# Attention stage: who copies the value product out of PSUM, VectorE or ScalarE

## The chip, the cores and the metric

The kernel runs on one core of a Trainium2 chip. The metric is the device time of one execution in microseconds (us). Engine names: TensorE (PE; its weight loads are a row of their own, PEld), VectorE (DVE), ScalarE (ACT), GpSimd (POOL) and SyncE (SP). A difference is told from none here from 0.2% on.

## The reference

Four graph layers run one after the other on x, of shape 128 batches x 128 nodes x 128 channels, each as `x = x + layer(relu(layernorm(x)))`. The second is the attention layer, the one that the change touches:

```python
qkv = x @ Wqkv
q, k, v = jnp.split(qkv, 3, axis=-1)
scores = jnp.einsum('btd,bsd->bts', q, k) * scale + adj_mask
scores = jnp.where(causal, scores, NEG)
attn = jax.nn.softmax(scores, axis=-1)
y = jnp.einsum('bts,bsd->btd', attn, v)
return y @ Wo
```

The first layer is a graph convolution with four small LSTMs, the third mixes three weight matrices by parts of the adjacency, the fourth is an edge attention.

## The kernel before, in words

The whole of x stays in SBUF. The attention stage works on 128 batches in 8 turns of 16 (`TURNS`, `NB`), each turn in 4 groups of 4 batches (`W1`, `QB`), so there are 32 groups. Query and key weights are multiplied ahead of time into one matrix `m_qk`, value and output weights into `w_vo`. All data of this stage are fp32. A group goes through these steps:

- `HT`: TensorE transposes the four normalised tiles (L820) into PSUM; ScalarE copies them with a relu to `hT1`.
- `QK`: the query product with `m_qk` (L826, one matmul of 512 columns); ScalarE copies it to `hmT`.
- `VAL`: the value product, `hT1` with `w_vo`, four matmuls (L831) into PSUM bank 2; it is copied to `val`. This copy is the subject.
- `SCORE`: four score matmuls (L837); VectorE adds the masked adjacency (L751) and takes the negated row maximum (L755).
- `EXP`: ScalarE takes four exponentials with row sums (L798).
- `PT`: TensorE transposes the exponentials (L843); ScalarE copies them to `probT`.
- `OUT1`: four matmuls of `probT` with `val` (L850); VectorE divides by the row sums and adds to x (L769, L775).
- `STATS` and `APPLY`: VectorE takes statistics of the turn after (L762, L107), GpSimd makes scale and shift and the normalised tiles (L727 to L740).

The three plain copies on ScalarE share one line, L786. The trace counts a matmul of fp32 data twice where it isn't a transpose, so four value matmuls are 8 in it.

Each engine runs the rounds in an order written out by hand. `IN_ROUND` is the order of TensorE, ScalarE and GpSimd, `ON_VECTOR` that of VectorE. An entry (step, d) means that in round r the step is done for group r - d. So in one round TensorE does HT of group r, PT of r-3, QK, VAL and SCORE of r-1 and OUT1 of r-3, and the EXP of a round is for group r-2. Engines are in step by semaphores only: `b_vp` says that the value product is there, `b_v` that it has been copied (the value product of the next round waits for it, since there is one bank, and so does OUT1 two rounds later), `b_e` that the exponentials are there (PT of the next round waits for it).

Of the kernel before, what the change touches and what calls it, by code (L numbers as in the profile page):

```python
# [21 lines left out]
def sync_names(nc, ctx, names):  # L22
    return {n: ctx.enter_context(nc.semaphore(n)) for n in names.split()}


def four_layers(nc, x_in, adj, adjT, Wg0, bg0, Wg1, bg1, WihT, WhhT, bihT, bhhT, WqkvT, Wo, W2, bias2,
# [11 lines left out]
    with ExitStack() as ctx:  # L38
# [65 lines left out]
        def norm_aggr(k, n, done):  # L104

            for j in range(k, k + n):
                nc.vector.bn_aggr(mv[:, j], stats[:, j]).then_inc(done, 1)  # L107
# [10 lines left out]
        def turn_start(i):  # L118

            return 0 if isinstance(i, int) and i == TURNS else i * NB  # L120
# [15 lines left out]
        def relu_norm(act, i, g, k, n):  # L136
# [3 lines left out]
            for j in range(g * GB + k, g * GB + k + n):  # L140
# [36 lines left out]
        S = sync_names(nc, ctx, "ld_e ld_x0 ld_lstm ld_w ld_x1 ld_x pool_made dve_made w_high w_low pool_link dve_link "  # L177
                                "act_link pe_srt pe_w pe_b0 pe_adj")
        with nc.Block() as block:

            @block.sync
            def _(sp):
                ends = ((ends_row[:, 0], src_row.to_broadcast([P, E])), (ends_row[:, 1], dst_row.to_broadcast([P, E])),
                        (ends_col[:, 0], src_col), (ends_col[:, 1], dst_col))
                for dst, s in ends:
                    sp.dma_start(dst, s).then_inc(S["ld_e"], 16)
                sp.dma_start(x[:, 0:NB, :], x_in[0:NB].rearrange("b t c -> t b c")).then_inc(S["ld_x0"], 16)
                for dst, s in ((w_raw[:, 0], WihT), (w_raw[:, 1], WhhT), (b_ih[:], bihT), (b_hh[:], bhhT)):
                    sp.dma_start(dst, s).then_inc(S["ld_lstm"], 16)
                for dst, s in ((adj_sb[:], adj), (adjT_sb[:], adjT), (w_g[:, 0], Wg0), (w_g[:, 1], Wg1),  # L190
                               (b0_col[:], bg0), (b1_bc[:], bg1.to_broadcast([P, P])), (a_sb[:], a_col),
                               (wqkvT[:], WqkvT.rearrange("(k d) c -> d k c", d=P)), (wo_sb[:], Wo),
                               (w2_sb[:], W2.rearrange("k f o -> f k o")),
                               (w_lv[:], WlvT), (w_out[:], WoutT),
                               (bias2_bc[:], bias2.to_broadcast([P, P]))):
                    sp.dma_start(dst, s).then_inc(S["ld_w"], 16)
                for i in range(1, TURNS):
                    sp.dma_start(x[:, i * NB:(i + 1) * NB, :],
                                 x_in[i * NB:(i + 1) * NB].rearrange("b t c -> t b c")).then_inc(
                                     S["ld_x1" if i == 1 else "ld_x"], 16)  # L200
# [253 lines left out]
        with nc.Block() as block:  # L454
# [121 lines left out]
            def _(pe):  # L576
# [48 lines left out]
                def item(i, g, n, more, before):  # L625
# [39 lines left out]
                    else:  # L665
# [13 lines left out]
        val = tmp("val", [P, W1, QB, C])  # L679
# [5 lines left out]
        S = sync_names(nc, ctx, "b_stats b_aggr b_var b_nmean b_rstd b_shift b_hn b_hTp b_hT b_qp b_q b_vp b_v b_sp b_s b_max b_e b_pTp "  # L685
                                "b_pT b_op b_inv b_o")
        HT, PT, QK, VAL, SCORE, OUT1, EXP, STATS, APPLY = range(9)


        IN_ROUND = [(HT, 0), (PT, 3), (QK, 1), (VAL, 1), (EXP, 2), (SCORE, 1), (STATS, 0), (OUT1, 3), (APPLY, 1)]  # L690
        ON_VECTOR = [(OUT1, 4), (STATS, 0), (VAL, 1), (SCORE, 1)]

        def pipeline(stage, beside):

# [18 lines left out]
        def bank(what, g):  # L713
            return ps[:, BANK[what][g % 2]]

        def by4(ap, n=QB):
            return ap.rearrange("p (b t) -> p b t", b=n)

        with nc.Block() as block:
# [25 lines left out]
            @block.vector  # L745
            def _(dve):
                def stage(i, what, g, more, before):
                    count = i * W1 + g + 1
                    if what == SCORE:
                        dve.wait_ge(S["b_sp"], count)  # L750
                        nc.vector.tensor_tensor(prob[:, g], by4(bank(SCORE, g)),  # L751
                                                adj_causal[:].unsqueeze(1).to_broadcast([P, QB, T]),
                                                ALU.add).then_inc(S["b_s"], 1)
                        dve.wait_ge(S["b_s"], count)
                        nc.vector.tensor_reduce(nmax[:, g * QB:(g + 1) * QB], prob[:, g], AXX, ALU.max,  # L755
                                                negate=True).then_inc(S["b_max"], 1)
                    elif what == VAL:
                        dve.wait_ge(S["b_vp"], count)
                        nc.vector.tensor_copy(val[:, g], by4(bank(VAL, g))).then_inc(S["b_v"], 1)
                    elif what == STATS:  # L760
                        for j in range(g * QB, (g + 1) * QB):
                            nc.vector.bn_stats(stats[:, j], x[:, turn_start(i + 1) + j]).then_inc(S["b_stats"], 1)  # L762
                        dve.wait_ge(S["b_stats"], count * QB)
                        if i > 0:
                            dve.wait_ge(S["b_shift"], count - W1)
                        norm_aggr(g * QB, QB, S["b_aggr"])
                    elif what == OUT1:
                        dve.wait_ge(S["b_e"], count)
                        nc.vector.reciprocal(rinv[:, g * QB:(g + 1) * QB], rsum[:, g * QB:(g + 1) * QB]).then_inc(  # L769
                            S["b_inv"], 1)  # L770
                        dve.wait_ge(S["b_op"], count)
                        dve.wait_ge(S["b_inv"], count)
                        for b in range(QB):
                            xs = x[:, i * NB + g * QB + b]
                            ins = nc.vector.scalar_tensor_tensor(xs, bank(OUT1, g)[:, b * C:(b + 1) * C],  # L775
                                                                 rinv[:, g * QB + b:g * QB + b + 1], xs,
                                                                 ALU.mult, ALU.add)
                        ins.then_inc(S["b_o"], 1)

                pipeline(stage, ON_VECTOR)  # L780

            @block.scalar
            def _(act):
                def copy(sem, count, dst, src, done, func=ACT.Copy):
                    act.wait_ge(sem, count)
                    nc.scalar.activation(dst, by4(src), func).then_inc(done, 1)  # L786

                def stage(i, what, g, more, before):
                    count = i * W1 + g + 1
                    if what == HT:  # L790
                        copy(S["b_hTp"], count, hT1[:, g], bank(HT, g), S["b_hT"], ACT.Relu)
                    elif what == QK:
                        copy(S["b_qp"], count, hmT[:, g], bank(QK, g), S["b_q"])
                    elif what == EXP:
                        act.wait_ge(S["b_max"], count)
                        for b in range(QB):
                            n = g * QB + b
                            ins = nc.scalar.activation(prob[:, g, b], prob[:, g, b], ACT.Exp, bias=nmax[:, n:n + 1],  # L798
                                                       accum_out=rsum[:, n:n + 1])
                        ins.then_inc(S["b_e"], 1)  # L800
                    elif what == PT:
                        copy(S["b_pTp"], count, probT[:, g], bank(PT, g), S["b_pT"])

                pipeline(stage, IN_ROUND)

            @block.tensor
            def _(pe):
# [5 lines left out]
                def stage(i, what, g, more, before):  # L813
# [31 lines left out]
                    elif what == OUT1:  # L845
                        pe.wait_ge(S["b_pT"], count)
                        pe.wait_ge(S["b_v"], count)
                        if count > 2:
# [14 lines left out]
        S = sync_names(nc, ctx, "c_stats c_aggr c_var c_rstd c_nmean c_shift c_hn c_hTp c_hTh c_hTl c_wp c_hw c_xb "  # L863
                                "c_own c_op c_o")
# [8 lines left out]
        with nc.Block() as block:  # L873
# [87 lines left out]
            def _(pe):  # L961
                def stage(i, what, g, more, before):
# [20 lines left out]
                    elif what == OUT2:  # L983
# [3 lines left out]
                        for k in range(2):  # L987
# [27 lines left out]
        S = sync_names(nc, ctx, "d_stats d_aggr d_var d_rstd d_nmean d_shift d_hn d_hTp d_hT d_xqp d_xvp d_xqh d_xql "  # L1015
                                "d_xv d_zp d_rl d_lr d_lgp d_logd d_logp d_log")
# [7 lines left out]
        with nc.Block() as block:  # L1024
# [78 lines left out]
            def _(pe):  # L1103
# [21 lines left out]
                for n in range(NG):  # L1125
# [23 lines left out]
                    if n == 0:  # L1149
# [15 lines left out]
        S = sync_names(nc, ctx, "e_lg e_fb e_m e_sub e_exp e_exTp e_ex e_denp e_inv e_att e_xvh e_xvl e_vp e_va "  # L1165
                                "e_yp e_y e_op e_o e_st")
# [187 lines left out]
```

## Time and profile before

| | |
|---|---|
| median of 3 runs | 1310.18 us (1309.94 to 1312.72) |
| the profiled execution | 1309.45 us |
| span of its trace, first to last instruction | 1307.6 us |
| busy over the span: TensorE, VectorE, ScalarE, GpSimd | 91%, 77%, 62%, 32% |
| attention stage, hT transposes of group 0 to the next stage's first | 737.3 to 889.8 us |

The profile is of one execution. Times in its rows are in us from the span's start unless they are called ns. The idle time in brackets is that of the engine ahead of the instruction, with an arrow to what ended it. The share of busy time over the whole span is a mean over four stages with different limits, so the attention stage has to be read by itself.

### The profile page before, as it was taken

The page shows a single profiled execution, that of the slowest core. Times are in us where ns is not written, and L with a number is a line of the kernel's source. Part 1 is how long each engine was busy: PE and PEld are TensorE (multiplying, and loading weights), DVE is VectorE, ACT ScalarE, POOL GpSimd, SP SyncE. Part 2 cuts the span into 40 slices and gives each one's busy share as a digit, 9 for nine tenths or more (in the row PEclk, how much of TensorE's full clock was granted, in tenths as well). Part 3 has the DMA queues.
Part 4 walks back from the last instruction along what each step waited for, and adds up shares of the span by engine and source line. Part 5 has one row for each costly group of instructions (what it writes and reads, how often), then busy time and mean ns, then how long its engine had stood idle before and what let it go on. Part 6 is the DMA issues. An engine that isn't in the chain of part 4 may idle for free. (4 is left out here: it accounts for less than half of the span.)

```text
span 1307.6 us, 24530 instructions
## 1 busy us (share of the span) xinstructions
PE 1192.5 (91%) x7808; PEld 1024.9 (78%) x7808; DVE 1010.0 (77%) x2796; ACT 812.9 (62%) x1804; POOL 412.6 (32%) x779
## 2 busy tenths in 40 slices
PE   2889999899899998998999799998999899968998
PEld 1678788787787886877878688886777688857997
DVE  6677877878778778777787699997777578775776
ACT  3477575775765757757667576776777376742332
POOL 3110200200102002001020277775767488832332
PEclk7899999999999999999999899999999899988999
DMA  9300000000000000000000000000000000001222
GB/s 269 93 1 1 1 1 1 0 0 0 0 0 0 0 0 0 0 0 0 0 1 1 1 2 2 2 2 1 1 1 1 1 1 2 2 1 40 72 72 72
DMA packets 24728, 21.09 MB, mean 16 GB/s; under 512 B 1744, under 2 KB 20304, under 8 KB 24400
## 3 DMA queue, kind: packets, MB, share of 16 engines
q1 hardware_dynamic: 24656, 20.21, 5.4%
q8 instruction: 36, 0.59, 0.2%
q14 instruction: 36, 0.29, 0.1%
HBM read 11.82 MB, written 8.39 MB: 15 GB/s over the span
## 5 line engine op out<-in xcount | busy, mean ns | idle before, releaser
L557 ACT ACTIVATE gate<-ps,b_lstm 128x256 f32<-128x256 f32 (+2 forms) x624 | 300.4, 558 | 36.8 <-PE ps L584 36.8
L582 PE MATMUL ps<-H_hi,w_hi 128*128 128x256 f32 (+2 forms) x624 | 212.4, 342 | 42.1 <-ACT gate L557 25.3
L583 PE MATMUL ps<-H_hi,w_lo 128*128 128x256 f32 (+2 forms) x624 | 205.3, 330 | 0.0
L584 PE MATMUL ps<-H_lo,w_hi 128*128 128x256 f32 (+2 forms) x624 | 195.9, 335 | 6.6 <-DVE H_lo L526 5.2
L126 POOL TENSOR_SCALAR rstd<-mv 128x8 f32<-128x8 f32 x18 | 12.3, 685 | 600.5 <-DVE mv L107 600.4
L582 PEld LDWEIGHTS ps<-H_hi,w_hi 128*128 128x128 f32 x624 | 117.5, 188 | 68.2 <-ACT gate L557 32.6
L567 ACT ACTIVATE tanh_c<-cell 128x512 f32<-128x512 f32 (+2 forms) x176 | 90.4, 514 | 127.6 <-DVE cell L517 81.7
L584 PEld LDWEIGHTS ps<-H_lo,w_hi 128*128 128x128 f32 x624 | 114.6, 189 | 25.1 <-DVE H_lo L526 17.5
L583 PEld LDWEIGHTS ps<-H_hi,w_lo 128*128 128x128 f32 x624 | 117.8, 189 | 7.6
L582 PE MATMUL ps<-hid_hi,w_hi 128*128 128x256 f32 (+2 forms) x384 | 119.0, 316 | 0.8 <-DVE hid_hi L523 0.8
L583 PE MATMUL ps<-hid_hi,w_lo 128*128 128x256 f32 (+2 forms) x384 | 117.3, 312 | 0.0
L584 PE MATMUL ps<-hid_lo,w_hi 128*128 128x256 f32 (+2 forms) x384 | 105.1, 314 | 0.7
L523 DVE TENSOR_TENSOR hid_hi<-gate,tanh_c 128x256 fp32r<-128x256 f32 (+2 forms) x96 | 47.8, 497 | 52.0 <-ACT tanh_c L567 52.0
L582 PEld LDWEIGHTS ps<-hid_hi,w_hi 128*128 128x128 f32 x384 | 72.7, 189 | 4.7 <-DVE hid_hi L523 1.4
L583 PEld LDWEIGHTS ps<-hid_hi,w_lo 128*128 128x128 f32 x384 | 72.8, 190 | 2.3
L141 ACT ACTIVATE hn<-x,shift,rstd 128x128 f32 (+1 forms) x144 | 64.6, 479 | 14.9 <-POOL shift L134 14.9
L1180 POOL TENSOR_TENSOR xv_lo<-xv,xv_hi 128x512 fp32r<-128x512 f32 x32 | 40.9, 1278 | 101.7 <-ACT xv_hi L1249 101.7
L584 PEld LDWEIGHTS ps<-hid_lo,w_hi 128*128 128x128 f32 x384 | 67.4, 189 | 6.3 <-DVE hid_lo L526 3.9
L1223 DVE TENSOR_TENSOR va<-ps,att 128x256 f32<-128x256 f32 x128 | 48.2, 419 | 27.8 <-PE ps L1287 27.7
L513 DVE TENSOR_TENSOR gate<-gate 128x256 f32<-128x256 f32 (+2 forms) x96 | 47.4, 494 | 27.6 <-ACT gate L557 27.6
L1295 PE MATMUL ps<-hot_sT,va 128*128 128x128 f32 x512 | 62.5, 275 | 0.5 <-DVE va L1223 0.5
L523 DVE TENSOR_TENSOR H_hi<-gate,tanh_c 128x512 fp32r<-128x512 f32 (+1 forms) x64 | 41.7, 652 | 27.1 <-ACT tanh_c L567 24.8
(206 smaller groups left out, 3102.8 us busy)
## 6 DMA issues: line engine op xcount, KB each, us to landing
out<-x SPq DMA_DIRECT2D x32, 256.0 KB, 2.3
w_raw<-in_WihT SPq DMA_DIRECT2D x1, 1024.0 KB, 8.6
w_raw<-in_WhhT SPq DMA_DIRECT2D x1, 1024.0 KB, 8.1
wqkvT<-in_WqkvT SPq DMA_DIRECT2D x1, 192.0 KB, 4.9
w_sb<-in_W SPq DMA_DIRECT2D x1, 192.0 KB, 4.6
ends_row<-in_src_row SPq DMA_DIRECT2D x1, 128.0 KB, 3.6
ends_row<-in_dst_row SPq DMA_DIRECT2D x1, 128.0 KB, 3.7
x<-in_x_in SPq DMA_DIRECT2D x8, 0.5 KB, 10.5
```

Source lines behind the costliest of these rows:

```text
L126: nc.gpsimd.tensor_scalar(r, mv[:, g * GB:(g + 1) * GB, 1], EPS, None, ALU.add).then_inc(sa(g, "a_var"), 1)
L141: nc.scalar.activation(hn[:, j], x[:, bass.ds(turn_start(i) + j, 1), :].rearrange("p a c -> p (a c)"), ACT.Relu, bias=shift[:, j:j + 1], s ...
L513: nc.vector.tensor_tensor(gi, gi, gg, ALU.mult).then_inc(sa(g, "a_part"), 1)
L523: nc.vector.tensor_tensor(h_hi, go, tc, ALU.mult).then_inc(sa(g, "a_hid"), 1)
L557: nc.scalar.activation(gate[:, g, z, 0:w * GB], gate_bank(g, k, m)[:, 0:w * GB], ACT.Tanh if z == G else ACT.Sigmoid, bias=b_lstm[:, 4 * ( ...
L567: nc.scalar.activation(tanh_c[:, g, 0:w * GB], cell[:, g, 0:w * GB], ACT.Tanh).then_inc(sa(g, "a_tanh"), 1)
L582: nc.tensor.matmul(dst, w_hi[:, src, p - 1, z], v_hi, start=start, stop=False)
L583: return nc.tensor.matmul(dst, w_lo[:, src, p - 1, z], v_hi, start=False, stop=False)
L584: return nc.tensor.matmul(dst, w_hi[:, src, p - 1, z], v_lo, start=False, stop=stop)
L1180: nc.gpsimd.tensor_tensor(xv_lo[:], xv[:, bass.ds(n * QB, QB), :].rearrange("p b c -> p (b c)"), xv_hi[:].bitcast(F32), ALU.subtract).then ...
L1223: nc.vector.tensor_tensor(va[:, c, k * HB:(k + 1) * HB].rearrange("p b (h d) -> p (b h) d", h=HEADS), ps[:, c, k * HB * C:(k + 1) * HB * C ...
L1295: ins = nc.tensor.matmul(ps[:, 6, b * T:(b + 1) * T], va[:, c, b], hot_sT[:, c], start=(c == 0), stop=(c == EC - 1))
```

## The change

The value copy goes from VectorE to ScalarE. `VAL` is taken out of `ON_VECTOR`; ScalarE, which runs `IN_ROUND`, now does something at the entry `(VAL, 1)`, which it passed over before. That entry stands behind `(QK, 1)` and ahead of `(EXP, 2)`. Semaphores, banks and buffers stay the same.

```diff
         IN_ROUND = [(HT, 0), (PT, 3), (QK, 1), (VAL, 1), (EXP, 2), (SCORE, 1), (STATS, 0), (OUT1, 3), (APPLY, 1)]
-        ON_VECTOR = [(OUT1, 4), (STATS, 0), (VAL, 1), (SCORE, 1)]
+        ON_VECTOR = [(OUT1, 4), (STATS, 0), (SCORE, 1)]
...
-                    elif what == VAL:
-                        dve.wait_ge(S["b_vp"], count)
-                        nc.vector.tensor_copy(val[:, g], by4(bank(VAL, g))).then_inc(S["b_v"], 1)
...
                     elif what == QK:
                         copy(S["b_qp"], count, hmT[:, g], bank(QK, g), S["b_q"])
+                    elif what == VAL:
+                        copy(S["b_vp"], count, val[:, g], bank(VAL, g), S["b_v"])
                     elif what == EXP:
                         act.wait_ge(S["b_max"], count)
```

## Rows read from the trace of the kernel before

**Rows 1.** Windows: busy us (instructions) by engine, granted clock, DMA share, GB/s.
```profile
core 0: us, PE busy (x) PEld busy (x) DVE busy (x) ACT busy (x) POOL busy (x), PEclk, DMA share, GB/s
796.00:814.00 18.00, 18.00 (x140) 16.09 (x138) 17.31 (x66) 12.97 (x45) 13.68 (x34) 1.00 0.00 1
```

**Rows 2.** Waits, 760 to 880 us: total, times, longest.
```profile
ACT hT L786 <- PE ps L820: 27.2, 26, 1.0
...
PEld ps L831 <- issue: 12.9, 54, 0.2
```

**Rows 3.** Timeline of one steady round: start, length, engine, line, operation, [idle before].
```profile
803.86 1.02 PE L826 MATMUL ps<-hT,m_qk 128*128 128x512 f32 x2
...
804.72 1.05 PE L831 MATMUL ps<-w_vo,hT 128*128 128x128 f32 x8
...
804.92 0.60 ACT L786 ACTIVATE hmT<-ps 128x512 f32<-128x512 f32 x1 [0.21 <-PE ps L826]
...
805.41 0.39 ACT L798 ACTIVATE prob<-prob,nmax 128x128 f32<-128x128 f32 x1
...
806.86 0.19 ACT L798 ACTIVATION_READ_ACCUMULATOR prob<-prob,nmax 128x1 f32 x1
...
807.79 0.47 PEld L843 LDWEIGHTS ps<-ident,prob 128*128 128x128 f32 x4
807.90 0.60 PE L843 MATMUL ps<-ident,prob 128*128 128x128 f32 x4
...
808.10 0.60 ACT L786 ACTIVATE hT<-ps 128x512 f32<-128x512 f32 x1 [1.05 <-PE ps L820]
...
808.33 1.02 PE L826 MATMUL ps<-hT,m_qk 128*128 128x512 f32 x2
```

**Rows 4.** Groups of instructions, 780 to 850 us: count, busy us, mean ns.
```profile
L759 DVE COPY val<-ps 128x512 f32<-128x512 f32 x15 | 9.9, 658 | 0.0
...
L786 ACT ACTIVATE hmT<-ps 128x512 f32<-128x512 f32 x16 | 9.6, 597 | 3.4 <-PE ps L826 3.4
```

**Rows 5.** Timeline of the first transposes of prob, which waited.
```profile
749.45 0.19 ACT L798 ACTIVATION_READ_ACCUMULATOR prob<-prob,nmax 128x1 f32 x1
...
749.68 0.66 PE L843 MATMUL ps<-ident,prob 128*128 128x128 f32 x4 [1.36 <-ACT prob L798]
...
750.18 1.02 PE L826 MATMUL ps<-hT,m_qk 128*128 128x512 f32 x2
750.38 0.60 ACT L786 ACTIVATE probT<-ps 128x512 f32<-128x512 f32 x1 [0.27 <-PE ps L843]
```

**Rows 6.** Timeline of the stage's last rounds.
```profile
875.43 1.02 PE L826 MATMUL ps<-hT,m_qk 128*128 128x512 f32 x2
...
879.47 1.02 PE L826 MATMUL ps<-hT,m_qk 128*128 128x512 f32 x2
...
880.33 1.05 PE L831 MATMUL ps<-w_vo,hT 128*128 128x128 f32 x8
...
881.42 0.69 DVE L759 COPY val<-ps 128x512 f32<-128x512 f32 x1 [0.36 <-PE ps L831]
...
883.07 0.60 PE L843 MATMUL ps<-ident,prob 128*128 128x128 f32 x4
...
883.71 0.60 ACT L786 ACTIVATE probT<-ps 128x512 f32<-128x512 f32 x1 [1.05 <-PE ps L843]
```

**Rows 7.** Timeline of the round with the first exponentials.
```profile
745.88 1.05 PE L831 MATMUL ps<-w_vo,hT 128*128 128x128 f32 x8
...
746.69 1.28 ACT L798 ACT_TABLE_LOAD   x1
```

**Rows 8.** Windows at the stage's start, columns as in the first group.
```profile
736.00:738.00 2.00, 0.67 (x4) 0.70 (x4) 1.68 (x6) 0.00 (x0) 0.00 (x0) 0.78 0.00 0
...
743.00:744.00 1.00, 1.00 (x6) 1.00 (x6) 0.33 (x1) 0.00 (x0) 1.00 (x4) 0.52 0.00 0
...
748.00:750.00 2.00, 0.64 (x6) 0.40 (x5) 1.97 (x6) 2.00 (x9) 1.86 (x5) 1.00 0.00 0
```

## The prediction

> **What bounds the kernel now.** I looked first at the attention stage alone, since the diff touches nothing else. The table of windows shows TensorE's matmul row full there, 18.00 of 18.00 us, VectorE at 17.31, ScalarE at 12.97, at a granted clock of 1.00 [rows 1]. Two full rows don't say which engine sets the pace, so the next view is that of waits over the whole steady part: the weight loads of TensorE wait only on "issue", never for VectorE, ScalarE or GpSimd, while ScalarE waits 27.2 us for the transposes on TensorE [rows 2]. So TensorE paces the round. The timeline gives its length: the query product (L826) starts at 803.86 and again at 808.33, 4.47 us apart; from 750.18 to 875.43 there are 28 such rounds, 4.473 us each [rows 3, 5, 6]. The reader is to see in the timeline that ScalarE, though idle 1.05 us a round ahead of its hT copy [rows 3], has its idle time at one place only, behind the exponentials.
>
> **What the edit costs on each engine.** VectorE loses 32 copies of 658 ns, 21.1 us in all; ScalarE gets 32 of the form that its hmT copy has, 597 ns [rows 4], 19.1 us. Both engines have room for their new sum, VectorE 17.31/18.00 x 4.47 - 0.66 = 3.64 us and ScalarE 12.97/18.00 x 4.47 + 0.50 = 3.72 us of 4.47 a round. So nothing follows from the totals; it is the order that decides.
>
> VectorE's relief is worth nothing. Its next operation, the score add, begins when the score product ends, which TensorE sets; TensorE's own waits for VectorE (b_s, two rounds back, and b_o, two rounds back) don't show in the waits [rows 2]. No wait on b_v is tight either: the value buffer is used two rounds later, and the next value product comes a round later.
>
> **What is now late on ScalarE.** In ScalarE's queue stand, in each round: hT copy, probT copy, hmT copy, [val copy], four exponentials. Behind the inserted copy wait the exponentials, and for these waits TensorE's transpose of prob (L843) of the next round. Take q as the start of the query product on TensorE, and read the offsets in [rows 3] (q = 803.86):
> - hmT copy starts at q+1.06. Exponentials start at q+1.55, 0.49 later (ScalarE starts the next 0.11 before the copy's end), and their last accumulator read ends at 806.86+0.19, q+3.19.
> - The next transposes of prob load weights at 807.79, q+3.93. Where this engine really waited for the exponentials, they began 0.04 to 0.05 behind the last read's end: 749.45+0.19 to 749.68 [rows 5], with the engine idle for 1.36 us before. So today there is 3.93 - 3.19 - 0.05 = 0.69 us of slack between exponentials and transposes.
> - The value product starts at 804.72, q+0.86, and its last matmul ends at +1.05, q+1.91. A copy that waits for it starts 0.04 later: 880.33+1.05 = 881.38, and VectorE's copy starts at 881.42 [rows 6]. So the val copy on ScalarE starts at q+1.95, not at q+1.55: ScalarE first stands 0.40 idle, for which there was no wait before. Then 0.49 to the exponentials: q+2.44, which is 0.89 later than now. End: q+4.08 (1.64 for the four, as now).
> - The transposes start at q+4.13, against the weight load at q+3.93 now. 0.89 is more than the slack of 0.69: TensorE now waits.
> - With the engine empty before, transposes to query product take 749.68 to 750.18 = 0.50 [rows 5] (0.43 in the full stream, 807.90 to 808.33 [rows 3]). So q' = q + 4.63.
>
> This is a closed loop, since the query product, the value product, the copy, the exponentials and the transposes each follow the one before; the slack is not used up once but each round gets 4.63 long in place of 4.47, **+0.16 us**. TensorE's order is fixed, so nothing fills the gap. Nothing else gets tight in it: the hT copy on ScalarE starts at q+4.24 as now, behind the last exponential, held by its transposes on TensorE (808.10 [rows 3]); probT's copy (transposes' start + 0.70, [rows 5]) starts at q+4.83 and is over before the next hmT copy at q'+1.06.
>
> **The ends of the pipeline**, where cover is thinner:
> - First exponentials: now the table load starts at 746.69, at once behind the hmT copy; the value product (745.88+1.05 = 746.93) ends later [rows 7]. The copy takes 746.97 to 747.57, the load starts at 747.58: 0.89 later. Exponentials and transposes follow directly here already [rows 5], so all of it counts: **+0.89**.
> - Then 28 rounds, query product 750.18 to 875.43 [rows 5, 6], of +0.16: **+4.5**.
> - The last round with a query product has no hT transposes and is 4.04 long (875.43 to 879.47 [rows 6]). The loop above doesn't run through the hT transposes, so it is 4.63 there too: **+0.59**.
> - In the next, transposes of prob start at 883.07, q+3.60 [rows 6]; they will at q+4.13, and their copy comes 0.70 instead of 0.64 behind the start: **+0.59**. After that no value copy is left, and the chain (copy, exponentials, transposes, product) runs as now.
>
> Sum: 0.89 + 4.5 + 0.59 + 0.59 = 6.6 us. The profiled execution took 1309.45 us (span 1307.6); 1316.0 after. The median of the three runs lies 0.73 above it, so 1316.7 us.
>
> Bounds of what the trace doesn't show, a copy of the values on ScalarE: duration between the hmT copy's 597 and VectorE's 658 ns, I take 597, the same shape on the same engine; at 658 the round is 0.06 longer, 28 x 0.06 + 0.2 = +1.9. The two-decimal offsets add up to about 0.03 a round, 0.8 us in all. The step from value product to copy is bounded by 0 below and by 0.05 above (the gap of [rows 5]). So 5.5 to 9.
>
> One rule speaks against the move itself. The value copy takes 658 ns on VectorE and its like 597 on ScalarE [rows 4]. The Trainium skill ("ScalarE: Activation LUTs", Rules for kernel authors) says to prefer VectorE over ScalarE for the simple operations; taken as no ScalarE copy beating VectorE's, it would give the upper case above, a sum of 8.5 instead of 6.6. The rows of this case don't agree with it for such a copy.
>
> A second rule touches the two hops between engines. The rows give 0.04 to 0.05 us for each [rows 5, 6]. The Trainium skill ("Advanced Engine Details and Errata", Network/Comms) gives 50-100 ns to read a semaphore; at 0.1 for both hops an estimate by that page is 0.11 a round more, a sum near 10. The trace is below it.
>
> **Rivals.**
> 1. *The cover holds (not slower).* If the value copy could start directly behind the hmT copy, the delay of the exponentials would be 0.49, under the slack of 0.69, and the steady round would stay 4.47. It decides at 0.69. Then only the ends pay: 0.5 at the table load and about 0.2 (q' = 1.06+0.50+0.49+1.64+0.05+0.50 = 4.24 against 4.04) in each of the last two: +0.9, 1311.1 us. For it: ends of matmuls are modelled. Against: VectorE's copies that waited for this product started 0.04 after the modelled end.
> 2. *The clock falls.* TensorE's idle time ahead of the first transposes of prob grows from 1.36 [rows 5] to 2.3 us. At the stage's start the clock fell (0.78, then 0.50 [rows 8]) while TensorE was busy 0.67 us out of 2. In the window with the present 1.36 it was busy 0.64 out of 2 and the clock stayed 1.00 [rows 8]. If it falls, a round with some 4.3 us of matmuls runs at the half level for as long as at the start, some 6 us (737 or 738 to near 744, with 0.52 in the last window), which costs up to 3 us less what the stall hides: 6.6 + 2.5, 1319.2 us.
> 3. *VectorE had been the real bound (faster).* If the 0.2 us by which the round exceeds 40 steps of the transposes' pace (four from 807.90 to 808.33 [rows 3], 0.107 each, 4.28) came from VectorE's load, the round would fall by 0.19, 28 x 0.19 = 5.3: 1304.9 us. Against: no wait for it [rows 2].
> 4. *Hops are dearer than read.* Both at 0.1 us: 28 x 0.11 + 0.3 more than mine, 1320.1 us.
>
> **Numbers.** Mine 0.74, cover holds 0.10, clock 0.09, hops 0.04, VectorE 0.03. A difference under 0.2%, 2.6 us, can't be told from none here. Mine, the clock and the hops all lie above it (0.87); cover holds lies within (0.10), VectorE below (0.03). The likeliest case's own range is 1315 to 1319; to leave out no more than 2 in 10 it reaches to 1313 and 1320.3, which takes in the clock and the hops and leaves out cover holds and VectorE.
>
> **What the profile after would show.** Query products 4.63 apart in the steady part; a new wait of the prob transposes (L843) for the exponentials in every round, some 0.2 us of idle on the weight-load row, about 29 times; a wait of ScalarE's val copy for the value product, 0.4 each; VectorE near 3.64 busy a round and waiting for the score product; the first table load 0.9 later; granted clock 1.00 from 744 on. Wrong would make me: no wait at L843 (the cover held), exponentials that don't move by 0.89, or a clock under 1.00 near 751.

## The result

| | runs | median | range |
|---|---|---|---|
| before | 4 | 1311.33 us | 1309.94 to 1312.72 |
| changed | 4 | 1320.7 us | 1320.26 to 1321.06 |

The ratio is 1.0071, 95% interval 1.0054 to 1.0089: slower by 0.7%, 9.4 us from median to median. The forecast was slower, 1316.7 us, with a range up to 1320.3; the time lies 0.4 us outside it. In later sessions the changed kernel ran 6 times more (median 1318.83, 8.25 over the kernel before there) and once (1320.45, 10.0 over), and 55 further runs of the kernel before spread over 1307.45 to 1312.63. So part of the miss varies with the execution; the rest are terms that the sum left out.

**The steady round after.** Windows of the changed kernel, as in [rows 1]:

```profile
core 0: us, PE busy (x) PEld busy (x) DVE busy (x) ACT busy (x) POOL busy (x), PEclk, DMA share, GB/s
796.00:814.00 18.00, 18.00 (x136) 15.63 (x135) 14.47 (x59) 15.42 (x48) 13.05 (x32) 1.00 0.01 1
```

VectorE fell from 17.31 to 14.47 and ScalarE rose from 12.97 to 15.42. TensorE's matmul row still reads full, since the modelled ends cover short gaps; its weight-load row fell from 16.09 to 15.63, and that is where the loss is seen. Waits, 760 to 870 us, as in [rows 2]:

```profile
POOL rstd L727 <- DVE mv L107: 27.9, 24, 4.8
DVE prob L751 <- PE ps L836: 16.9, 24, 0.7
PEld ps L830 <- issue: 11.5, 48, 0.2
ACT val L783 <- PE ps L830: 7.0, 24, 0.3
ACT hmT L783 <- PE ps L825: 6.1, 23, 0.3
PEld ps L842 <- ACT prob L797: 4.2, 24, 0.2
ACT hT L783 <- PE ps L819: 3.7, 24, 0.2
```

Three waits are new in this list: ScalarE's val copy waits 0.3 us a round for the value product, TensorE's transposes of prob wait 0.2 for the exponentials, and VectorE, which has less to do, waits 0.7 for the score product. GpSimd waits for VectorE's statistics, as it did before (23.0 us in 27 waits); nothing in the list waits for GpSimd. The timeline of a round, to be laid beside [rows 3] (q = 804.20):

```profile
804.20 1.02 PE L825 MATMUL ps<-hT,m_qk 128*128 128x512 f32 x2
...
805.06 1.05 PE L830 MATMUL ps<-w_vo,hT 128*128 128x128 f32 x8
...
805.26 0.60 ACT L783 ACTIVATE hmT<-ps 128x512 f32<-128x512 f32 x1 [0.26 <-PE ps L825]
...
806.15 0.60 ACT L783 ACTIVATE val<-ps 128x512 f32<-128x512 f32 x1 [0.29 <-PE ps L830]
...
806.65 0.39 ACT L797 ACTIVATE prob<-prob,nmax 128x128 f32<-128x128 f32 x1
...
808.10 0.19 ACT L797 ACTIVATION_READ_ACCUMULATOR prob<-prob,nmax 128x1 f32 x1
...
808.34 0.42 PEld L842 LDWEIGHTS ps<-ident,prob 128*128 128x128 f32 x4 [0.17 <-ACT prob L797]
...
808.83 1.02 PE L825 MATMUL ps<-hT,m_qk 128*128 128x512 f32 x2
```

The val copy starts at q+1.95, the exponentials at q+2.45, their last read ends at q+4.09, the transposes begin at q+4.14 and the next query product at q+4.63: the forecast's 1.95, 2.44, 4.08, 4.13 and 4.63.

**Behind the first exponentials.** The same kernel where TensorE's wait is long, as in [rows 5] and [rows 7]:

```profile
748.32 1.28 ACT L797 ACT_TABLE_LOAD   x1
...
751.32 0.66 PE L842 MATMUL ps<-ident,prob 128*128 128x128 f32 x4 [2.26 <-ACT prob L797]
...
751.81 1.67 PE L825 MATMUL ps<-hT,m_qk 128*128 128x512 f32 x2
...
753.27 1.92 PE L830 MATMUL ps<-w_vo,hT 128*128 128x128 f32 x8
...
757.90 1.02 PE L825 MATMUL ps<-hT,m_qk 128*128 128x512 f32 x2
```

```profile
752.00:754.00 2.00, 2.00 (x6) 1.07 (x6) 0.00 (x0) 1.08 (x2) 1.77 (x5) 0.51 0.00 0
754.00:756.00 2.00, 2.00 (x13) 2.00 (x13) 0.00 (x0) 0.89 (x3) 1.54 (x4) 0.63 0.00 0
```

TensorE stood idle for 2.26 us instead of 1.36, and behind it the granted clock is 0.51 and 0.63, the level of 1.2 GHz for most of 4 us. The value product takes 1.92 us in place of 1.05, and this round is 6.09 us long where the next are 4.63: **1.46 us** that the sum did not have.

**The start of the third stage.** First the changed kernel, then the one before:

```profile
898.54 1.68 PE L969 MATMUL ps<-ident,hn 128*128 128x128 f32 x8 [1.49 <-PEq L719]
...
904.78 1.03 PE L969 MATMUL ps<-ident,hn 128*128 128x128 f32 x4
```

```profile
889.87 1.06 PE L970 MATMUL ps<-ident,hn 128*128 128x128 f32 x8 [1.48 <-PEq L719]
...
894.13 0.60 PE L970 MATMUL ps<-ident,hn 128*128 128x128 f32 x4
```

From the first transposes to the second it takes 6.24 us against 4.26. In the changed kernel the clock is low there too (0.57 in the first 2.2 us). Nothing in that stage was changed.

**Where the 10.6 us between the two profiled spans (1318.2 and 1307.6) come from:** the attention stage began 0.65 later (737.98 against 737.33); it is 160.56 long against 152.54, +8.02, of which 1.46 is the clock behind the exponentials, 0.09 the clock at the stage's start, and 6.47 the order on ScalarE, forecast at 6.55; the stages behind it take 419.66 against 417.73, +1.93, about what the third stage's first interval differs by (1.98). The profiled executions themselves are 11.24 us apart (1320.69 and 1309.45): 0.64 lies outside the spans, and neither it nor the 0.65 ahead of the stage was explained.

### The profile page after: what moved, and what is told of

Same layout as the page of the kernel before. It is cut to its first block and busy times, and to the rows that moved or that the text cites. A ratio compares the mean times of both kernels' runs of the same rounds, so it can differ in the third digit from the quotient of the medians.

```text
span 1318.2 us, 24530 instructions
## 1 busy us (share of the span) xinstructions
PE 1202.2 (91%) x7808; PEld 1028.3 (78%) x7808; DVE 990.8 (75%) x2764; ACT 836.1 (63%) x1836; POOL 413.0 (31%) x779
```

## The experiments

A stage's length is taken from its first hT transposes to the first transposes of the next stage, in each kernel's profile. This takes out what differs in the rest of the kernel. The columns between are: start (first hT transposes to the second query product), first exponentials (second to fourth query product), the steady round, and the third stage's first interval.

| kernel | stage | start | first exp. | round | third stage |
|---|---|---|---|---|---|
| before | 152.54 | 7.68 | 9.64 | 4.47 | 4.26 |
| changed | 160.56 | 7.77 | 12.15 | 4.63 | 6.24 |
| changed, second profile | 160.64 | 7.66 | 12.35 | 4.63 | 4.24 |
| changed, third profile | 160.76 | 7.78 | 12.35 | 4.63 | 6.50 |
| changed, wait filled | 158.93 | 7.60 | 10.69 | 4.63 | 4.23 |
| changed, wait filled, again | 159.09 | 7.78 | 10.68 | 4.63 | 5.59 |
| exponentials first | 151.40 | 6.54 | 9.64 | 4.47 | 6.42 |
| before + one copy | 153.59 | 7.78 | 10.15 | 4.47 | 6.16 |
| before + two copies | 162.35 | 6.40 | 10.98 | 4.78 | 5.66 |
| before + two copies, again | 162.34 | 6.38 | 10.99 | 4.78 | 5.70 |
| changed, early table | 157.60 | 7.78 | 9.25 | 4.63 | 6.50 |
| exponentials first, early table | 151.11 | 7.68 | 8.21 | 4.47 | 5.80 |
| the same, start filled | 148.39 | 4.95 | 8.21 | 4.47 | 5.60 |
| the same, both ends filled | 148.39 | 4.95 | 8.21 | 4.47 | 4.25 |

### The value copy on ScalarE, behind the exponentials

```diff
+        ON_SCALAR = [(HT, 0), (PT, 3), (QK, 1), (EXP, 2), (VAL, 1)]
...
-                pipeline(stage, IN_ROUND)
+                pipeline(stage, ON_SCALAR)
```

> ScalarE still makes the value copy, but behind the four exponentials instead of ahead of them. Theory A (the order is what costs, not the engine: the exponentials stand behind a wait for the value product and come out past the slack of 0.69 us): the exponentials start at q+1.55 again, the transposes of prob don't wait in the steady part, the round is 4.47 us, and no clock drop follows the first exponentials; within 0.2% of before, 8 to 10 us under the changed kernel. Theory B (ScalarE's added work as such, 0.5 us a round, or the loss of the copy on VectorE slows the round): the round stays near 4.63 us and the time within 3 us of the changed kernel.

Measured: 1309.5 us (11 runs) against 1310.14 us for before (22 runs), ratio 0.9991 (0.9981 to 1.0001). ScalarE in a steady round:

```profile
755.79 0.60 ACT L784 ACTIVATE hmT<-ps 128x512 f32<-128x512 f32 x1 [0.21 <-PE ps L826]
756.28 0.39 ACT L798 ACTIVATE prob<-prob,nmax 128x128 f32<-128x128 f32 x1
...
757.73 0.19 ACT L798 ACTIVATION_READ_ACCUMULATOR prob<-prob,nmax 128x1 f32 x1
757.82 0.57 ACT L784 ACTIVATE val<-ps 128x512 f32<-128x512 f32 x1
758.96 0.60 ACT L784 ACTIVATE hT<-ps 128x512 f32<-128x512 f32 x1 [0.57 <-PE ps L820]
```

The same engine does the same copy, but in the idle time ahead of hT's copy, of which 0.57 is still left, and without a wait for the value product. The round is 4.47, so theory B falls: neither ScalarE's added work nor anything that VectorE lost costs time. Against the kernel before in its own session this one is 0.6 us faster, within the noise, where the changed kernel is 8.25 to 10.0 slower; the whole loss hangs on the order of two entries in a list. The stage is 1.14 us shorter than before, all of it at its start (6.54 against 7.68), where the clock fell later. VectorE's relief is worth nothing either: it was busy 15.08 of 18.00 us here, where it had been 17.31, and the round didn't get shorter.

### How much delay the exponentials bear

```diff
                         copy(S["b_qp"], count, hmT[:, g], bank(QK, g), S["b_q"])
+                        if count > 1:
+                            act.wait_ge(S["b_spare"], 1 * (count - 1))
+                        nc.scalar.activation(spare[:, 0, 0:512], same[:].rearrange("p a e -> p (a e)")[:, 0:512], ACT.Copy).then_inc(S["b_spare"], 1)
```

The semaphore only orders the spare copy behind the one of a round earlier, which is long done. The second kernel has two such copies.

> The kernel before (value copy on VectorE) with one spare ScalarE copy of 128x512 from SBUF, which waits for nothing, between hmT copy and exponentials. It delays the exponentials by 0.49 to 0.55 us, under the slack of 0.69. Theory A (threshold): the round stays 4.47 us, only the ends pay, about 0.5 + 0.2 + 0.2: +0.9 us over before. Theory B (each added 0.5 us of ScalarE ahead of the exponentials is paid in part): the round grows by 0.1 or more, +3 us or more.

> The same with two spare copies, none of which waits: the delay is 0.98 to 1.1 us, past the slack. Theory A: round q+1.06+3x0.49+1.64+0.05+0.50 = 4.72 us (up to 4.85 if a copy from SBUF takes longer), +0.25 to +0.38 a round; sum 0.98 + 28x0.25 + 2x0.68 = +9.3 us, up to +13, over before, and the clock may drop behind the first exponentials as in the changed kernel, for 1.5 us more. A theory that the wait for the value product itself (not the delay) is the harm expects no growth of the round here.

ScalarE in a steady round, first with one spare copy, then with two:

```profile
765.98 0.60 ACT L787 ACTIVATE hmT<-ps 128x512 f32<-128x512 f32 x1 [0.21 <-PE ps L830]
766.47 0.62 ACT L797 ACTIVATE spare<-same 128x512 f32<-128x512 f32 x1
766.99 0.39 ACT L802 ACTIVATE prob<-prob,nmax 128x128 f32<-128x128 f32 x1
```

```profile
767.06 0.60 ACT L787 ACTIVATE hmT<-ps 128x512 f32<-128x512 f32 x1 [0.26 <-PE ps L831]
767.56 0.62 ACT L797 ACTIVATE spare<-same 128x512 f32<-128x512 f32 x1
768.08 0.62 ACT L798 ACTIVATE spare<-same 128x512 f32<-128x512 f32 x1
768.60 0.39 ACT L803 ACTIVATE prob<-prob,nmax 128x128 f32<-128x128 f32 x1
```

A spare copy holds the exponentials back by 0.52. One leaves the round at 4.47; two, 1.04, make it 4.78, which is 1.06 + 0.49 + 1.04 + 1.64 + 0.05 + 0.50, the loop of the forecast. With two, the wait list from 760 to 870 us has

```profile
PEld ps L848 <- ACT prob L803: 7.4, 23, 0.3
```

and with one it has no such line. So there is a threshold between 0.52 and 1.04 (below 0.89, since the changed kernel is past it), and a plain delay without any wait for the value product is enough to pass it. The stage with one copy is 1.05 us longer than before, 0.10 of it at the start; expected was 0.9. With two it is 9.8 longer while its start was 1.28 shorter, 11.1 in all: 28 x 0.31 + 1.04 + 2 x (4.78 - 4.04) = 11.2. In both kernels that pass the threshold the round grows by the delay less 0.73 (1.04 - 0.31 and 0.89 - 0.16): the weight load begins to wait at 0.69, and 0.04 comes back behind it, since from the transposes to the query product it takes 0.50 after a wait and 0.54 from the weight load without one (807.79 to 808.33 in [rows 3]).

The times: 1313.12 us with one copy (10 runs, ratio 1.0017, 1.0007 to 1.0026), 1323.07 with two (4 runs, 1.0096, 1.0081 to 1.0112), 12.9 over before and so within the 9.3 to 13 expected. The first is 3.0 over the median of before, 2 more than its stage gives. Its profile has the slow start of the third stage; whether it has that more often than the kernel before wasn't shown.

### The changed kernel once more

> The changed kernel once more, with its own profile and more runs. My sum by the order on ScalarE was +6.55 us; the first profile had 1.46 us more from a clock at the half level in the fourth round and 1.93 us more from one at the start of the third stage. Theory A (the order's part is fixed, the clock's part comes and goes from execution to execution): rounds 4.63 apart again, the stage 159.1 us long plus or minus the clock terms, and runs spread over 1316 to 1321 us. Theory B (the clock drops come with the change each time): both drops are there again, and the runs stay within 0.5 us of 1320.7.

> The changed kernel, a third profile. The clock's drop behind the first exponentials was in both profiles so far (1.46 and 1.66 us more in the two rounds behind them), that at the start of the third stage in one of two. If the first comes with the change, it is there a third time, 1.4 to 1.7 us; if it is chance, it may be absent. Rounds 4.63 apart in any case.

Measured: 1318.83 us (6 runs, 1316.31 to 1320.17) against 1310.58 (23 runs), ratio 1.0068 (1.0054 to 1.0082); then 1320.45 once. Neither theory holds whole. The clock's drop behind the first exponentials is in all three profiles: 1.46, 1.66 and 1.66 us over the 10.69 that the order alone gives (5.17 + 0.89 + 4.63). The slow third stage is in two of three, and also in kernels whose order is harmless, such as the one with the exponentials first. So the first comes with this kernel each time and the second comes and goes. The kernel before has one profile only, without the second; how often it has it isn't known. The second profile, without the latter, took 1316.31 us: 6.86 over the profiled execution of before, less than the 8.1 of its stage, since it entered the stage 0.14 earlier and what follows the stage was 1.0 shorter.

### Filling the wait

```diff
                     elif what == PT:
+                        if count == 1:
+                            for _ in range(2):
+                                nc.tensor.matmul(bank(PT, g), m_qk[:], hT1[:, 0].rearrange("p b t -> p (b t)"),
+                                                 start=True, stop=True)
                         pe.wait_ge(S["b_e"], count)
```

> The changed kernel, with two query-like matmuls of 512 columns (1.7 us, results overwritten) that TensorE does only once, in its idle 2.3 us ahead of the first transposes of prob. Theory A (idle time there lets the clock fall from 752 to 755.6 us in the trace, and the half clock costs 1.5 us): the clock stays 1.00 there, the next round is 4.63 instead of 6.09 us long, and the attention stage gets 1.46 us shorter. Theory B (the long round comes from something else, such as the later table load): it stays near 6.1 us. The total falls by 1.5 us, or by 3.4 if the clock at the start of the third stage holds too.

> The changed kernel with the wait ahead of the first transposes of prob filled by two matmuls, a second profile. If the filling keeps the clock, it is 1.00 there again and the first two rounds behind the exponentials are 6.06 and 4.63 long as in its first profile; if that profile was luck, the drop may appear, +1.5.

Measured: 1315.58 us (5 runs), ratio to before 1.0037 (1.0024 to 1.005), 5.4 over before where the changed kernel was 8.25 to 10.0 over in its sessions; its profile has the third stage at full clock too. The one run of the second session took 1318.19, 7.7 over, with a slow third stage. TensorE in the first:

```profile
747.48 1.88 PE L841 MATMUL ps<-hT,m_qk 128*128 128x512 f32 x4
749.90 0.66 PE L846 MATMUL ps<-ident,prob 128*128 128x128 f32 x4 [0.54 <-ACT prob L797]
750.39 1.02 PE L825 MATMUL ps<-hT,m_qk 128*128 128x512 f32 x2
```

Windows from those transposes on, in the first profile and in the second:

```profile
749.90:755.00 5.10, 5.10 (x38) 4.45 (x39) 1.54 (x4) 4.12 (x13) 3.91 (x10) 1.00 0.01 3
```

```profile
751.97:757.00 5.03, 5.03 (x38) 4.38 (x39) 1.47 (x4) 4.05 (x13) 3.92 (x10) 1.00 0.01 3
```

The transposes begin 5.57 us behind the second query product (744.33 to 749.90), as in the changed kernel (745.75 to 751.32), and yet the intervals between query products around them are 6.06 and 4.63 in both profiles, where the changed kernel has 6.06 and 6.09. So 1.5 to 1.7 us of the loss is the clock and not the order. What is left once the difference at the stage's start is taken out, 158.93 - 152.54 + 0.08 = 6.47 and 159.09 - 152.54 - 0.10 = 6.45 us, is the order's part by itself, against the 6.55 forecast.

> The kernel before with two spare copies, a second profile. Its first had TensorE idle for 2.40 us ahead of the first transposes of prob, as long as in the changed kernel, and no drop of the clock. If such a wait is enough for a drop at some times and not at others, the drop may be there now, +1.5; if something in the changed kernel other than the wait makes it, it is absent again. Rounds 4.78 apart.

Measured: 1322.75 us, no drop again, although TensorE was idle there for 2.40 us:

```profile
751.01 0.66 PE L848 MATMUL ps<-ident,prob 128*128 128x128 f32 x4 [2.40 <-ACT prob L803]
751.51 1.02 PE L831 MATMUL ps<-hT,m_qk 128*128 128x512 f32 x2
```

So a wait of this length does not by itself bring the clock down. These two profiles also have a short stage start (6.4 us). Among those with the long start of 7.6 to 7.8, waits of 0.83 and 1.36 us were followed by no drop, nor was the wait of 1.88 in the kernel with one spare copy, and the wait of 2.26 was, three times:

```profile
751.01 0.66 PE L847 MATMUL ps<-ident,prob 128*128 128x128 f32 x4 [1.88 <-ACT prob L802]
```

Whether what went before at the stage's start decides the drop, or something else in these kernels does, can't be said from these runs.

### The exponential's table, loaded early

```diff
                 interleave(act, [(item, 0, 0), (gates, 0, 0), (cell_tanh, 0, 0),
                                  (item, 1, 1), (gates, 1, 1), (cell_tanh, 1, 1)])
+                nc.scalar.activation(warm[:], half[:, 0:1], ACT.Exp)
```

> The changed kernel with the exponential's table loaded at the end of the first stage, where ScalarE is idle (one exponential of a constant column ahead of the attention stage). The first exponentials then stand behind the val copy alone, at 747.46 in the clock of the profile before, 1.4 us earlier than in the changed kernel; TensorE's idle time ahead of the first transposes falls from 2.3 to about 1.0 us. Theory A (the wait there is table load plus delay, and the clock fell for the idle time): sum 6.55 - 1.4 = +5.1 us over before, and the clock stays 1.00 behind them. If the clock's drop there doesn't depend on that wait, it is there again, +1.5.

> Value copy on ScalarE behind the exponentials, and the early table. Rounds 4.47 apart; the first transposes of prob wait next to nothing, so the stage is 1.4 us shorter than before: -1.4 us (1308.7 where before has 1310.1). A theory that the table load is hidden expects no difference from the kernel with the exponentials first.

Measured: with the changed order 1318.01 us (4 runs, ratio 1.0054, 1.0033 to 1.0074); with the exponentials first 1309.76 (12 runs, 0.9994, 0.9985 to 1.0004). In the stage alone both came as worked out: 157.60 is 5.06 over before (5.1 expected), 151.11 is 1.43 under (1.4 expected). In the changed order the wait ahead of the transposes is 0.83 us instead of 2.26, and no drop follows:

```profile
749.39 0.66 PE L844 MATMUL ps<-ident,prob 128*128 128x128 f32 x4 [0.83 <-ACT prob L799]
749.89 1.02 PE L827 MATMUL ps<-hT,m_qk 128*128 128x512 f32 x2
```

Over whole executions 1.4 us can't be told from nothing here. The changed order with the early table is 7.4 over before, 2.4 more than its stage gives; its profile has the slow third stage (6.50).

### Filling TensorE's waits at both ends

```diff
+                def filler():
+                    nc.tensor.matmul(ps[:, 0], ident[:], same[:].rearrange("p a e -> p (a e)"), start=True, stop=True)
...
+                        if isinstance(i, int) and i == TURNS and g == 1:
+                            filler()
...
                 interleave(pe, [(input_share, 0, 0), (input_share, 1, 1), (item, 0, 0), (item, 1, 1)])
+                filler()
```

The results of these matmuls are overwritten unread. Both kernels have the value copy behind the exponentials and the early table. The last kernel has, on top, one of 256 columns ahead of each of the last two output products and one of 512 behind the last.

> The same with two 512-column matmuls on TensorE (results overwritten) in its idle times of 1.4 and 1.5 us at the end of the first stage, ahead of and behind its last transposes. If TensorE's idle time there lets the clock fall (half level from 738 to 744 us in the profile before, 4.8 us of matmuls at half speed), the stage's start to the query product of the third round falls by up to 2.4 us below the version without. If the clock falls all the same, no difference, or a loss of up to 0.3 us where the filler delays the stage's end.

> Value copy behind the exponentials, early table, fillers at the end of the first stage, and now also three at the end of the attention stage (two of 256 columns, one of 512, in TensorE's waits there). If idle time at the end of the stage lets the clock fall at the start of the third (first interval of its transposes 5.6 us in the version without, 4.24 where the clock holds), the third stage gains up to 2 us in the executions that had the drop, about 1 in the median: 1307 us where the version without has 1308.1. If it can't be held so, or the fillers delay the last waits, the same as without or 0.3 longer.

Measured: 1308.1 us (12 runs) against 1310.58, ratio 0.9984 (0.9975 to 0.9993); both ends 1306.76 us (6 runs) against 1310.45 (10 runs), 0.9968 (0.9956 to 0.998). The window over the stage boundary, where the kernel before has 0.78 and 0.52 [rows 8], in the kernel with its start filled:

```profile
730.00:744.00 14.00, 11.96 (x74) 8.94 (x75) 9.40 (x33) 7.35 (x17) 5.00 (x12) 1.00 0.00 0
```

The clock never fell, and the start is 4.95 us instead of 7.68, 2.7 less where up to 2.4 was expected. With both ends filled the third stage starts at full clock in the one profile:

```profile
887.40:889.40 2.00, 1.03 (x8) 0.79 (x8) 0.74 (x2) 1.08 (x2) 1.22 (x1) 1.00 0.00 0
```

This alone doesn't show that the fillers at the end hold the clock, since three profiles without them started the third stage at full clock as well (4.23 to 4.26), and the two kernels' intervals against before overlap.

The kernel with both ends filled is 3.7 us under before in its session, and 12 to 14 under the changed kernel's medians of the others. The gain isn't that of the copy's move: with the exponentials first and nothing else the time is that of before. In the stage, 1.4 us of it comes from the early table and 2.7 from the filled start. Neither was tried with the copy left on VectorE.

## Why the prediction was off, point by point

- **TensorE sets the round**: right. Giving VectorE 0.66 us a round more room changed nothing (exponentials first, 4.47).
- **Slack of 0.69 us between exponentials and transposes, delay 0.89**: right. 0.52 didn't lengthen the round, 1.04 did, and the changed kernel's offsets agree to 0.01 us with the forecast's. The wait of ScalarE's val copy reads 0.29 and not 0.4, because the forecast counted from where the next instruction could have started and the trace counts from the end of the copy ahead; it is the same start at q+1.95.
- **Busy time of a round**: a little low, without effect. Over 23 rounds of the changed kernel (767.16 to 873.65) VectorE is busy 3.75 us a round and ScalarE 3.92, against 3.64 and 3.72. Both stay under the 4.63.
- **A closed loop of 4.63 us, 28 times, and the ends**: right, 6.45 to 6.47 us with the clock's part taken out against 6.55 summed. The 28 rounds brought 4.39 of it (4.5 forecast, with 4.473 taken as 4.47). The last round with a query product is 4.63 long (882.91 to 887.54), as forecast.
- **ScalarE's copy at 597 ns and the hops at 0.04 to 0.05 us**: right. The copy's mean is 597 ns from 780 to 850 us. The value product ends at 806.11, by its modelled end, and the copy starts at 806.15; the last read of the exponentials ends at 808.29 and the weight load starts at 808.34. The Trainium skill ("Advanced Engine Details and Errata", Network/Comms) gives 50-100 ns for the reading of a semaphore; this trace has 0.04 and 0.05 us from end to start, at or under the lower figure. The Trainium skill's preference for VectorE in simple operations ("ScalarE: Activation LUTs", Rules for kernel authors) is stated for relu, max, min, add and mul, not for a copy, and this copy isn't dearer on ScalarE: it is 0.60 here and was 0.66 on VectorE.
- **The table load**: the 0.89 of the first exponentials was right. The Trainium skill ("ScalarE: Activation LUTs", What ACT_TABLE_LOAD costs) puts a drain of about 1380 ns beside a load of 1283. The load here is 1.28, the first exponential starts 0.02 behind it, and loading early brought 1.4 us, so no drain of that size was on the path.
- **The step that failed: "granted clock 1.00 from 744 on", and with it the chance of 0.09 for the fall of the clock.** It was kept as a rival and put at nothing in the sum, though the forecast itself had lengthened TensorE's wait from 1.36 to 2.3 us, in the very stage where [rows 8] show a clock of 0.78 and 0.52 around waits of that engine. The fall was there in three profiles out of three, at 1.46 to 1.66 us (the rival's price was 2.5). With it the sum is 1310.18 + 6.5 + 1.6 = 1318.3, which the stated range still holds; so this step accounts for a part of the miss only.
- **What the range left out besides**: the same clock at the start of the third stage, +1.93 us in the profile. The forecast looked at the attention stage alone, "since the diff touches nothing else", and so put every other stage at nothing. From profile to profile the miss is 1320.69 - 1316.0 = 4.7 us: 1.46 behind the exponentials, 1.93 at the third stage, 0.09 at the stage's start, 0.65 ahead of it and 0.64 outside the spans, less 0.08 on the order's part. The last two sizes stay open, and so does whether the third stage's 1.93 comes from the change: the changed kernel has it in two profiles of three, and harmless orders have it too. A single profile of before without it, beside three runs, made the reference look firmer than it is: its runs reach from 1307.45 to 1312.72. Had the time come out 0.5 us lower, within the range, that would have been luck, since the clock's terms would have been missing all the same.

## What to carry to other kernels

Moving an operation to a less busy engine is decided by its place in that engine's queue: work out what stands behind it, what that work's slack is, and what the operation itself has to wait for, since the wait is added to its length. If the delay passes the slack and the path closes on itself, the excess is paid in each round, here 0.16 us 28 times; two swapped entries made the loss vanish. And a longer wait of TensorE has to be priced with its clock: a few matmuls whose results nobody reads, put in such waits, brought 2.7 us at the stage's start and 1.5 to 1.7 behind the first exponentials, where the move of the copy brought nothing in either order.

## What the runs showed of the hardware

- Two matmuls of 512 columns in a wait of 2.3 us kept the granted clock at 1.00 twice, where without them it fell to the 1.2 GHz level three times out of three. A wait of 1.88 us in a second kernel and one of 2.40 in a third (twice) were followed by no fall. What tells these apart stays open.
- At the two stage boundaries the clock cost 2.7 us (start 7.68 against 4.95) and 2.0 (first interval 6.24 against 4.26). The first was in every profile without the filled start, at 1.4 to 2.8 us; the second in 10 of 14 profiles, at 1.3 to 2.3.
- A full busy row of TensorE hid a wait of 0.17 us in each round; the weight-load row and the list of waits showed it.
